# Last layer: its 4 MB of expert weights are loaded behind the first alibi maxima, its projection weights stay ahead of the last rope sequence

## The reference, cut to what matters

```
xn = layernorm(x)
s  = attn_l(xn)             # layer 0: selective scan, 1: causal, 2: rope, 3: alibi
g  = silu(ffn_l(xn))        # a mixture of experts
x  = x + s * g
```

## Time and profile before

| | |
|---|---|
| median of 3 runs | 1912.78 us (1908.93 to 1914.64) |
| the profiled execution, its own time | 1910.01 us |
| its span in the trace | 1907.9 us |
| PE busy | 1550.4 us (81%) |
| DVE busy | 1177.3 us (62%) |
| ACT busy | 1016.4 us (53%) |
| POOL busy | 209.0 us (11%) |
| DMA moved | 116.30 MB, mean 61 GB/s |
| mean granted TensorE clock | 0.864 of full speed |

### The profile page before, as it was taken

The page is one execution under the profiler, slowest core; times in us unless marked ns, Lnnn a source line. Parts: engine busy times, 40 slices in busy tenths (PEclk is TensorE's granted clock), DMA queues, the critical chain, the costliest instruction groups (busy, mean ns, idle before and its releaser), DMA issues. The chain is left out here.

```text
span 1907.9 us, 23980 instructions
## 1 busy us (share of the span) xinstructions
PE 1550.4 (81%) x8656; PEld 779.0 (41%) x8656; DVE 1177.3 (62%) x2370; ACT 1016.4 (53%) x1658; POOL 209.0 (11%) x152
## 2 busy tenths in 40 slices
PE   5999989898699688977889778887487577888886
PEld 2555555555455344433444333443132222323442
DVE  4789989999755742456533665324423777776522
ACT  4787777866033157633666326764575023334675
POOL 1342242432000000000000000000000000001003
PEclk9999999999899798878998789987657558888999
DMA  4432232352301210203002030004212122122002
GB/s 170 115 79 67 78 79 78 88 152 78 101 19 50 81 37 1 73 11 100 19 1 75 9 100 19 18 1 148 66 34 83 34 80 62 34 64 60 1 2 72
DMA packets 91621, 116.30 MB, mean 61 GB/s; under 512 B 10096, under 2 KB 71536, under 8 KB 91120
## 3 DMA queue, kind: packets, MB, share of 16 engines
q1 hardware_dynamic: 89808, 110.05, 20.1%
q0 software_dynamic: 1696, 4.72, 0.9%
HBM read 83.27 MB, written 31.46 MB: 60 GB/s over the span
## 5 line engine op out<-in xcount | busy, mean ns | idle before, releaser
L1661 ACT ACTIVATE scratch<-ps 128x1024 f32<-128x1024 f32 x272 | 270.5, 1022 | 197.1 <-PE ps L1263 63.6
L2075 DVE TENSOR_REDUCE neg_max<-ps 128x2 f32<-128x1024 f32 (+2 forms) x224 | 234.3, 1067 | 96.8 <-PE ps L1207 96.1
L1644 ACT ACTIVATE ps<-ps 128x512 f32<-128x512 f32 x256 | 150.1, 586 | 86.0 <-PE ps L1253 85.7
L1932 DVE TENSOR_TENSOR_SCAN scratch<-scratch 128x512 f32<-128x512 f32 x128 | 159.5, 1285 | 3.6 <-ACT scratch L1615 3.5
L1840 DVE SCALAR_TENSOR_TENSOR gated<-tanh,ps 128x512 f32<-128x512 f32 x88 | 60.4, 687 | 144.4 <-ACT tanh L1543 144.3
L1543 ACT ACTIVATE tanh<-ps 128x512 f32<-128x512 f32 x88 | 52.3, 595 | 159.0 <-PE ps L988 158.7
L1307 PE MATMUL ps<-scratch,values 128*32 128x512 f32 (+3 forms) x1024 | 131.4, 604 | 3.2 <-ACT scratch L1661 1.6
L1023 PE MATMUL ps<-xnt,weights_even 128*128 128x512 f32 x256 | 126.7, 617 | 7.4 <-ACT gated L1526 6.6
L2255 POOL TENSOR_SCALAR variance_eps<-mean_var 128x4 f32<-128x4 f32 x20 | 5.3, 265 | 1002.6 <-DVE mean_var L1760 1002.6
L988 PE MATMUL ps<-xnt,weights_odd 128*128 128x512 f32 x176 | 109.6, 708 | 0.0
L991 PE MATMUL ps<-xnt,weights_odd 128*128 128x512 f32 x176 | 98.7, 644 | 7.0 <-DVE values L2057 7.0
(11 more groups left out here) (323 smaller groups left out, 2975.5 us busy)
## 6 DMA issues: line engine op xcount, KB each, us to landing
scratch<-state_rows SPq DMA_DIRECT2D x64, 512.0 KB, 4.7
scratch<-parts_scratch SPq DMA_DIRECT2D x288, 96.0 KB, 2.3
parts_scratch<-weights_even SPq DMA_DIRECT2D x168, 128.0 KB, 2.4
weights_odd<-in_l SPq DMA_DIRECT2D x8, 519.5 KB, 6.4
weights_even<-in_l SPq DMA_DIRECT2D x1, 4096.0 KB, 15.6
weights_odd<-in_l SPq DMA_DIRECT2D x1, 4096.0 KB, 14.7
parts_scratch<-gated SPq DMA_DIRECT2D x15, 128.0 KB, 2.4
slots_scratch<-head_out SPq DMA_DIRECT2D x5, 256.0 KB, 5.3
```

Of the source, the lines that this page charges most:

```text
L1644: ins = act.activation(bank, bank, ACT.Exp, accum_out=dens[:, j, h:h + 1])
L1661: act.activation(dst, src, ACT.Exp).then_inc(q[l, "exp_done"], 1)
L1932: dve.tensor_tensor_scan(hs[:, g, :], da[n % RING][:, g, :], ub[:, g, :], 0.0, ALU.mult, ALU.add)\
L2075: ins = dve.tensor_reduce(dst, ps[:, base:base + 2, col:col + n], AX.X, ALU.max, negate=True)
```

## The change

Layer 3's weights are no longer loaded by one function. At the old place (between layer 1's end and the parts of layer 2's last sequence) SP loads only the front part, 834 columns, 417 KB. The other 8192 columns, the 4 MB of the experts, are issued behind `maxima(3, 0)`, that is once layer 3's first maxima have landed in SBUF. The front part gets a semaphore of its own, `front_weights_in`, shared with layer 0's front part (16 for layer 0, 32 for layer 3). PE, ACT and DVE wait on it for the first projection, and PE waits for the 4 MB (`s_w[3]`) at the first expert step, "eu" with n = 0. Layer 2's loads are the same DMAs through another function. The waits on layer 0's front part are renamed and keep their counts.

```diff
--- before.py
+++ after.py
@@ -784,10 +784,12 @@
 
         s_x = [sem("x_in%d" % b) for b in range(NB)]
         s_c32, s_c16 = sem("consts_in"), sem("consts16_in")
-        s_w = [sem(f"weights_in{l}") for l in range(4)]
+
+        s_front = sem("front_weights_in")
+        s_w = {l: sem(f"weights_in{l}") for l in range(1, 4)}
         rows_in = [sem("state_rows_in%d" % n) for n in range(RING)]
         s_experts = sem("experts_in0")
-        all_in = {1: 16 * 9, 2: 48, 3: 32}
+        all_in = {1: (s_w[1], 16 * 9), 2: (s_w[2], 48), 3: (s_front, 32)}
         s_out = sem("out_written")
         dl = sem("vector_own")
         pl = sem("pool_own")
@@ -1398,7 +1400,7 @@
                         expert_down(n - 1)
                     elif what == "q":
                         if n == 0 and b == 0:
-                            pe.wait_ge(s_w[l], all_in[l])
+                            pe.wait_ge(*all_in[l])
                         if n == 0:
                             pe.wait_ge(xnt_ready[before[l]], b + 2)
                         pe.wait_ge(*mi_read)
@@ -1453,6 +1455,7 @@
                         bank_read[route_bank(n)] = (q[3, "slots_turned"], n + 1)
                     elif what == "eu":
                         if n == 0:
+                            pe.wait_ge(s_w[3], 16)
                             pe.wait_ge(q[3, "slots_turned"], ST // 4)
                         for e in (2 * n, 2 * n + 1):
                             pe.wait_ge(*bank_read[route_bank(e)])
@@ -2302,16 +2305,14 @@
 
         @block.sync
         def _(sp):
-            def load_weights(l):
-
-                base = wb if l % 2 else wa
+            def rope_weights():
+
+                l = 2
                 cut = at[f"l{l}"]["w1"][0]
                 n = wide[f"l{l}"]
-                src = blobs[f"l{l}"]
-                sp.dma_start(base[:, 0:cut], src[:, 0:cut]).then_inc(s_w[l], 16)
-                sp.dma_start(base[:, cut:n], src[:, cut:n]).then_inc(s_w[l], 16)
-                if l == 2:
-                    sp.dma_start(wa[:, n:n + 2 * T], blobs["rope"]).then_inc(s_w[l], 16)
+                load_columns(l, 0, cut, s_w[l])
+                load_columns(l, cut, n, s_w[l])
+                sp.dma_start(wa[:, n:n + 2 * T], blobs["rope"]).then_inc(s_w[l], 16)
 
             def load_columns(l, lo, hi, landed):
 
@@ -2342,7 +2343,7 @@
                         load_columns(1, w * (s - 4), min(w * (s - 3), wide["l1"]), s_w[1])
 
             sp.dma_start(x[:, 0:TB, :], x_in_v[:, 0:TB, :]).then_inc(s_x[0], 16)
-            load_columns(0, 0, at["l0"]["w1"][0], s_w[0])
+            load_columns(0, 0, at["l0"]["w1"][0], s_front)
             sp.dma_start(c32[:, :], blobs["c32"]).then_inc(s_c32, 16)
             for b in range(1, NB):
                 sp.dma_start(x[:, TB * b:TB * (b + 1), :], x_in_v[:, TB * b:TB * (b + 1), :]).then_inc(s_x[b], 16)
@@ -2430,7 +2431,7 @@
                         for g in range(QUADS):
                             causal_stack(0, g)
                         sp.wait_ge(xn_ready[0], NB)
-                        load_weights(2)
+                        rope_weights()
                 elif what == "ld":
                     if l == 1:
                         causal_stack(b, n)
@@ -2440,7 +2441,7 @@
                     maxima(1, b)
                 elif what == "t" and l == 1 and n == 3 and b == NB - 1:
                     sp.wait_ge(xn_ready[1], NB)
-                    load_weights(3)
+                    load_columns(3, 0, at["l3"]["w1"][0], s_front)
                     rows(3)
             for n in range(2):
                 part_out(3, 0, n)
@@ -2453,6 +2454,7 @@
                 part_out(3, 1, n)
             last_stacks(1)
             maxima(3, 0)
+            load_columns(3, at["l3"]["w1"][0], wide["l3"], s_w[3])
             for b in range(2, NB):
                 for n in range(2):
                     part_out(3, b, n)
```

More of the change, by code:

```diff
@@ L1342, in attention @@
                         if b == 0 and k == 0:
-                            pe.wait_ge(s_w[0], 16)
+                            pe.wait_ge(s_front, 16)
                         if what == "hx":
@@ L1718, in attention @@
                         if n == 0 and b == 0:
-                            act.wait_ge(s_w[l], all_in[l])
+                            act.wait_ge(*all_in[l])
                         queries_keys(l, b, n)
@@ L1739, in _ @@
                 act.sem_inc(xnt_ready[n], 1)
-            act.wait_ge(s_w[0], 16)
+            act.wait_ge(s_front, 16)
             act.activation(small[:, 16:48], W(0, "a_log"), ACT.Exp).then_inc(q[0, "a_exp"], 1)
@@ L1897, in constants0 @@
                 l = 0
-                dve.wait_ge(s_w[0], 16)
+                dve.wait_ge(s_front, 16)
                 own.add(dve.memset(xp[:, :, 0:KC - 1], 0.0))
@@ L2158, in attention @@
                     elif what == "set":
-                        dve.wait_ge(s_w[l], 32)
+                        dve.wait_ge(s_front, 32)
                         ts(small[:, 48:49], W(l, "bq"), float(DH) ** -0.5, None, ALU.mult)\
@@ L2174, in attention @@
                         if n == 0 and b == 0:
-                            dve.wait_ge(s_w[l], all_in[l])
+                            dve.wait_ge(*all_in[l])
                         if l == 1 and n == 0 and b == 0:
```

## The result

The changed kernel takes 1904.04 us (median of 19 runs, 1897.22 to 1916.43), the kernel before 1914.64 us in its 19 runs beside it (1908.84 to 1921.31). The ratio is 0.9948, its 95% interval 0.9934 to 0.9962: 10 us less, between 7.3 and 12.6. The prediction said 1906.6 in a range of 1901.5 to 1912.0, and gave 0.50 to a gain of more than 0.3%. Way and range were right.

The account below looks back on a forecast made before the run. No engine was full (PE busiest at 81%); a chain of waits changing engines set the end. The terms, 6.2 us from DVE's wait and the rest 0, gave 1906.6 us on the median's scale, range 1901.5 to 1912.

Parts of the forecast that it names:

- Step 1: Layer 2's last sequence: without the 4 MB ahead, operand 0's parts land earlier and DVE's cast of operand 2 moves 6.3 us.
- Step 2: DVE's next check, for operand 3 on operand 1's parts: nearly all the gain is kept, 6.2 us, at worst 5.5.
- Step 3: Stacked operands of layer 2's last sequence: their read-back and PE's need at 1358 move by the same amount, worth nothing.
- Step 4: Alibi rows and slopes ahead of the parts: issued 0.4 us earlier, through by about 1320.5; cost 0, bound 1 us.
- Step 5: The 4 MB behind layer 3's first maxima: 45 us of empty queue for a 14.7 us transfer; cost 0.
- the 3 us that I allowed: Sign to check: from PE's transposes of the last xn to the end it takes 550.9 us as before, within 3.
- Step 6: Semaphores: one more wait on PE at the experts, long met, and the others only renamed; 0.
- The sum: All steps together: -6.2 us, from 1910.01 to 1903.8 in the profiled execution, 1906.6 us on the median's scale.
- the clock: Rival after 1333: four matmul blocks change clock level, 3.2 us either way, 1909.8 or 1903.4; chance of giving back 0.15.
- The rival on the slower side: An instruction fetch waits behind the 4 MB at its new place, 12.3 us late: 1918.9; chance 0.07, shared with larger clock loss.

Follow-up runs that it names:

- spare_parts: Kernel before, 4 MB at its old place, but operands 2 and 3 of layer 2's last sequence use layer 1's free part buffers, without DVE's check: ratio 0.9969.
- tail_at_six: Changed kernel with the third rope sequence's last step moved behind the first six score units of the last one: ratio 0.9926 to the kernel before.
- behind_parts: Changed kernel with the 4 MB issued right behind the last part of the last rope sequence, ahead of its stacked operands: ratio 0.9972 to the kernel before.
- two_mb_stay: Changed kernel with half of the 4 MB (w1, 4096 columns) kept at the old place: ratio 0.9971 to the kernel before.
- at_seq2_parts: Changed kernel with the 4 MB issued 45 us later, right ahead of the alibi parts of sequence 2: ratio 0.9959 to the kernel before.
- spare_again: The same kernel as spare_parts, timed again on one chip with the changed kernel: ratio 0.9959 to the kernel before.
- rename_only: Kernel before with only the new semaphores and PE's new wait, the 4 MB at its old place: ratio 1.0003 to the kernel before.

## Why the prediction was right, step by step

**Step 1, the load leaves its place: right.** I said that the cast moves by 6.3 us and that 0.65 us of gap, ACT's copy, remain. Measured: F fell by 6.3 and the gap is 0.72, released by ACT. spare_parts shows the path from the other side.

**Step 2, DVE keeps it: right, at the upper end.** I subtracted 0.1 for operand 3's check and gave a bound of 0.8; operand 1's parts landed in 2.3 to 2.5 us and the second cast followed without a gap.

**Step 3, the stacks move along at no cost: right**, and with more slack than I knew. The prediction named only that PE asks for them at 1358; tail_at_six showed 8.8 us between their landing and PE's first use. It was this slack that I undersized in behind_parts.

**Step 4, rows and slopes: right for this kernel.** No operand landed late. With 2 MB ahead of them, in two_mb_stay, they had not been through when the parts came, and 1.1 us of the wait stayed; so the bound of 1 us had a reason.

**Step 5, no cost at the new place: right.** No wait of PE, DVE or ACT names the load. The transfer took 13.0 us, not 14.7, and at_seq2_parts issues it 45 us later at the same ratio. The last stretch, from the transposes to the end, grew by 2.4 us; that is within the 3 us that I allowed, and spare_again shows that the part of it behind the token write does not come from the load.

**Step 6, semaphores at nothing: right** (rename_only, 1.0003).

**The sum was too small.** -6.2 us was forecast, 10 measured (7.3 to 12.6), and some 8 is the average over the six timings with the short F; the traces show 7.3. The term that was mis-sized is the clock, which I carried at zero with 3.2 us to either side, four blocks of 0.8 us. I named the mechanism and took its mean as nothing; the traces show one such block, the eight matmuls of L1307, and part of the next on the higher level with every short F, 1.1 us in the favourable way. The page of the Trainium skill that I weighed there (TensorE: Matmul & The Clock Gate, What's actually happening: the window runs free of the work) is in line with levels that differ over identical work, as in the first projection (5.60 and 6.71 us). It would also have let me expect scatter behind the transposes, where five traces agree within 0.1 us (82.9 to 83.0); no run here isolates it. I also wrote that PE's idle stretches move along and that one shrinks from 8.64 to 2.4 us; it shrank to 2.58, and I drew nothing from it. Whether it is what changes the level later on is not shown.

**The rival on the slower side**, an instruction fetch behind the 4 MB, did not come true. One fetch packet (q14) falls into the 13 us of the transfer in the changed kernel, so there was an occasion; the longest idle time of any engine there that names nothing is 0.8 us, and the ratio is the same at two places of the load.

**The chances.** I gave 0.50 to more than 0.3%. By DVE's gap alone the gain is 0.33%, with the change of level 0.38%, so it was a close call. That it came out as clearly as 0.52% was luck: the part of it that is shown beyond the gap I had sized at zero, and the rest is not explained.

## What to carry to other kernels

A large load on a queue that also carries small, timely transfers costs what the first wait behind it lacks in slack, not its own length: here 4 MB of 13 to 15 us cost 6.3 us at one place, 2.3 at another and nothing that shows at two others, and half of it cost 1.1 at the first place. So look for the check that stands behind the queue (here a buffer used by operand k and k + 2), and either move the load to a stretch where the queue is empty or give the check another buffer; both gave the same time. Then look at what the freed engine was hiding: the same stretch held another 5.4 us in the order of steps, which no transfer had caused.

## What the runs showed of the hardware

- The 4 MB load (128 rows of 32 KB, issued by SP) landed in 14.7 us with the rows, slopes and parts behind it, in 13.9 us with the stacks behind it (behind_parts), and in 13.0 us alone.
- Transfers on SP's queue waited for what stood ahead of them: parts of 128 KB landed in 2.3 to 2.8 us on a free queue, in 3.2 to 4.1 behind 2 MB, rows and slopes, and in 7.4 to 9.3 behind 4 MB, rows and slopes.
- The same eight matmuls took 1.93 us at a granted clock of 1.2 GHz and 1.06 at 2.4 GHz, and a shift of 6.3 us upstream was enough to move them from one level to the other, in five traces of five.
- The same kernel's time varies between runs by more than this change is worth, and its mean granted clock with it. The kernel before gave 1911.48 us at 0.865 and 1924.60 us at 0.857 on one chip. Two executions of equal code were already 1.1 us apart within the first eight matmuls of layer 0 (5.60 and 6.71 us), and 4.0 us apart at the front weights' issue. A difference of 0.3% in this kernel can't be read from two traces, and hardly from one set of timings; the length of a stretch can, if it is short and near the change: F came out at 38.9 us in five traces.
